# A grouped expert feed-forward kernel: weight loads move from once per expert to once per block, x arrives transposed, the work between the engines is dealt out anew

## The reference

```python
Wi_b = Wi[expert_idx]      # (E, 256, 1024) -> one per sample; bi, Wo (E, 1024, 256), bo, gamma, beta alike
h = gelu(einsum('bsh,bhi->bsi', x, Wi_b) + bi_b, approximate=False)
o = einsum('bsi,bih->bsh', h, Wo_b) + bo_b
r = o + x
y = (r - mean(r)) * rsqrt(var(r) + 1e-12)
return y * gamma_b + beta_b
```

## Time and profile before

| | |
|---|---|
| median of 3 runs | 149.77 us |
| the three runs | 149.15, 149.77, 151.67 us |
| span of the profiled execution, first to last instruction | 147.0 us |
| the median less that span (entry and exit) | 2.8 us |
| TensorE busy | 118.9 us (81%) |
| VectorE busy | 115.8 us (79%) |
| ScalarE busy | 76.2 us (52%) |
| GpSimd busy | 68.8 us (47%) |
| moved by DMA | 25.03 MB, 170 GB/s over the span |

### The profile page before, as it was taken

The page is one execution under the profiler, slowest core; times in us unless marked ns, Lnnn a source line. Parts: engine busy times, 40 slices in busy tenths (PEclk is TensorE's granted clock), DMA queues, the critical chain, the costliest instruction groups (busy, mean ns, idle before and its releaser), DMA issues.

```text
span 147.0 us, 3876 instructions
## 1 busy us (share of the span) xinstructions
PE 118.9 (81%) x949; PEld 116.1 (79%) x949; DVE 115.8 (79%) x181; ACT 76.2 (52%) x126; POOL 68.8 (47%) x57
## 2 busy tenths in 40 slices
PE   0296968998999999497999979993999399977800
PEld 0195968997999999496999979992999299977800
DVE  2493457178988998995999699969996999679880
ACT  3022966677089408547933990299129912970000
POOL 3006570217614962404492659255925593570220
PEclk9999999999999999999999999999999968999995
DMA  4979996999818210293947488756124612020021
GB/s 108 384 214 357 342 322 139 287 384 302 327 37 276 57 36 18 72 379 98 311 84 303 113 282 264 245 119 233 34 71 121 211 33 66 13 60 18 0 55 36
DMA packets 17710, 25.03 MB, mean 170 GB/s; under 512 B 1616, under 2 KB 14480, under 8 KB 17552
## 3 DMA queue, kind: packets, MB, share of 16 engines
q10 hardware_dynamic: 9824, 14.42, 30.3%
q1 hardware_dynamic: 7856, 10.26, 23.1%
HBM read 22.58 MB, written 2.10 MB: 168 GB/s over the span
## 4 chain that ended last, share of the span: by engine, by line
issue 50%; POOL 20%; DMA 12%; POOLq 7%; SPq 6%; DVE 2%; DVEq 0%; PE 0%
POOL wo_lo L344 14%; DMA x_in<-x_dram 6%; POOL xs L355 6%; DMA bo_bc<-L_cond_bo_dram 5%; SPq L214 5%; POOLq L224 3%; POOLq L355 1%; DMA idx_i<-itok_B_dram 1%; SPq L224 1%; POOL rstd L362 1%; POOLq L56 1%; SPq L181 0%; POOLq L373 0%; POOLq L383 0%; POOLq L372 0%
## 5 line engine op out<-in xcount | busy, mean ns | idle before, releaser
L344 POOL TENSOR_TENSOR wo_lo<-wo_in,wo_hi 128x1024 fp32r<-128x1024 f32 x15 | 43.7, 2932 | 22.7 <-ACT wo_hi L425 22.7
L696 PE MATMUL preact<-xT_hi,wi_hi 128*128 128x256 f32 x144 | 42.1, 292 | 11.6 <-DVE wi_lo L569 6.1
L436 ACT ACTIVATE h<-preact,biT 128x256 f32<-128x256 f32 x72 | 28.3, 484 | 41.3 <-DVE h_lo L596 29.2
L596 DVE TENSOR_TENSOR h_lo<-h,h_hi 128x512 fp32r<-128x512 f32 x36 | 47.4, 1357 | 0.6 <-ACT h_hi L444 0.6
L696 PE MATMUL preact<-xT_lo,wi_hi 128*128 128x256 f32 x144 | 41.5, 288 | 0.0
L696 PE MATMUL preact<-xT_hi,wi_lo 128*128 128x256 f32 x144 | 41.4, 288 | 0.0
L696 PEld LDWEIGHTS preact<-xT_hi,wi_hi 128*128 128x128 f32 x144 | 28.3, 196 | 13.0 <-issue 13.0
L696 PEld LDWEIGHTS preact<-xT_hi,wi_lo 128*128 128x128 f32 x144 | 28.4, 197 | 0.0
L696 PEld LDWEIGHTS preact<-xT_lo,wi_hi 128*128 128x128 f32 x144 | 28.3, 197 | 0.0
L713 PE MATMUL sums_ps<-wo_hi,h_hi 128*128 128x256 f32 x144 | 23.9, 288 | 1.7 <-DVE r L537 1.6
L362 POOL TENSOR_TENSOR rstd<-var_eps,minus_half 128x2 f32<-128x2 f32 x9 | 8.6, 953 | 34.7 <-DVE var_eps L550 34.7
(11 more groups left out here) (57 smaller groups left out, 74.9 us busy)
## 6 DMA issues: line engine op xcount, KB each, us to landing
wo_in<-L_cond_Wo_dram ACTq DMA_DIRECT2D x7, 1024.0 KB, 6.1
wi_in<-L_cond_Wi_dram ACTq DMA_DIRECT2D x5, 1024.0 KB, 5.2
wi_in<-L_cond_Wi_dram SPq DMA_DIRECT2D x3, 1024.0 KB, 9.4
x_in<-x_dram SPq DMA_DIRECT2D x36, 64.0 KB, 2.8
y_dram<-xs SPq DMA_DIRECT2D x32, 64.0 KB, 2.1
bo_bc<-L_cond_bo_dram SPq DMA_DIRECT2D x1, 1024.0 KB, 7.0
wo_in<-L_cond_Wo_dram SPq DMA_DIRECT2D x1, 1024.0 KB, 6.6
gamma_bc<-L_cond_gamma_dram ACTq DMA_DIRECT2D x3, 256.0 KB, 5.6
```

The lines of the kernel that those rows point to most:

```text
L344: nc.gpsimd.tensor_tensor(wo_half(wo_lo, e, half), wo_half(wo_in, e, half), wo_half(wo_hi, e, half).bitcast(FP32), ALU.subtract).then_inc( ...
L436: nc.scalar.activation(h[:, c, :], preact_chunk(c), ACT.Gelu, bias=biT[:, bass.ds(e * IC + c, 1)]).then_inc(gelu_done, 1)
L596: nc.vector.tensor_tensor(piece(h_lo, i), piece(h, i), piece(h_hi, i).bitcast(FP32), ALU.subtract).then_inc(h_lo_done, 1)
L696: last = nc.tensor.matmul(preact_chunk(c), w[:, e % 2, k, c * P:(c + 1) * P], xT[:, k, :], start=(k == 0 and w is wi_hi and xT is xT_hi), ...
```

## The change

- **Blocks unrolled.** The loops over experts and blocks become straight code for blocks 0 to 7 and nested conditions for the rest. Each block loads its own `wi`, `wo` and a row of parameters (`bo`, `gamma`, `beta`, `bi`), whether or not it shares the expert with the block ahead. The host lays the weights, parameters and x out in the order in which SBUF wants them.
- **x transposed.** The host gives x a second time, transposed (`x_columns`), so that TensorE's transposes and their PSUM bank go; each block loads four 64 KB pieces of it besides the four of `x_rows` for the residual.
- **Shorter sort.** Seven dependent steps with two waits for TensorE in place of fifteen. Table entries are now single sample numbers, read by one `value_load` each; places without a sample point to zero rows behind x, and every place is stored, with no conditions.
- **Queues.** All loads and stores of x, the weights and the parameters from the second block on are issued by SyncE; ScalarE's queue issues only the first block's `wi`, half of its x and its `wo`.
- **TensorE.** A quarter of the first product of block t (two chunks) alternates with a quarter of the second product of block t-1.
- **GELU in PSUM.** ScalarE writes GELU back to the bank it read; rounding (`h_high`) and subtraction (`h_low`) read PSUM. The SBUF copy `h` goes.
- **Subtractions.** `wo_lo` moves from GpSimd to VectorE; GpSimd keeps the residual bias and the root, now one per tile.

```diff
-            for (tile, half), b in samples.items():
-                eng.dma_start(x_tile(t, tile)[half * S:(half + 1) * S, :],
-                              x[bass.ds(b, 1), :, :].rearrange("o s h -> (o s) h")).then_inc(
-                                  first_x_loaded if is_first(t) else x_loaded, 16)
...
+        def entry(eng, at, hi, lo=0):
+            return eng.value_load(table[0:1, at:at + 1], min_val=lo, max_val=hi)
+
+        def sample(eng, t, j):
+            return entry(eng, QUAD * t + j, ROWS - 1)
...
+        def load_wi(eng, t, e):
+            if t >= 2:
+
+                eng.wait_ge(wi_lo_done, wi_count(t - 2, len(wi_pieces(t - 2)) - 1))
+            eng.dma_start(wi_in[:, t % 2, :, :, :].rearrange("p c k n -> p (c k n)"),
+                          wi[bass.ds(e, 1), :, :].rearrange("o p f -> (o p) f")).then_inc(wi_loaded[t % 2], 16)
...
+        def load_xT(eng, t, slots=range(QUAD)):
+            if t >= 2:
+                eng.wait_ge(x_ready, t - 1)
+            for j in slots:
+                b = sample(eng, t, j)
+                eng.dma_start(xT_in[:, t % 2, j, :, :].rearrange("p k s -> p (k s)"),
+                              xt[bass.ds(b, 1), :, :].rearrange("o p f -> (o p) f")).then_inc(xT_loaded[t % 2], 16)
+
+        def load_x(eng, t):
+            if t >= X_RING:
+                eng.wait_ge(stored[t % X_RING], 4 * loads_of(t - X_RING, X_RING))
+            for j in range(QUAD):
+                b = sample(eng, t, j)
+                eng.dma_start(slot(t, j), xr[bass.ds(b, 1), :, :].rearrange("o s h -> (o s) h")).then_inc(
+                    x_loaded[t % X_RING], 16)
+
+        def store(eng, t, tile):
+            eng.wait_ge(y_ready, 2 * t + tile + 1)
+            for j in (2 * tile, 2 * tile + 1):
+                b = sample(eng, t, j)
+                eng.dma_start(out[bass.ds(b, 1), :, :].rearrange("o s h -> (o s) h"), slot(t, j)).then_inc(
+                    stored[t % X_RING], 16)
...
+            sp.wait_ge(table_ready, 1)
+            load_xT(sp, 0, (0, 1))
+            second = expert(sp, 1)
+            load_wi(sp, 1, second)
+            load_xT(sp, 1)
+            load_params(sp, 1, second)
+            load_x(sp, 0)
+            load_wo(sp, 1, second)
+            load_x(sp, 1)
+            n = entry(sp, T_BLOCKS, MAX_BLOCKS, MIN_BLOCKS)
+
+            def iteration(t, ahead):
+                if ahead:
+                    e = expert(sp, t + 2)
+                    load_xT(sp, t + 2)
+                    load_wi(sp, t + 2, e)
+                    load_params(sp, t + 2, e)
+                    load_x(sp, t + 2)
+                if t >= 2:
+                    store(sp, t - 2, 1)
+                if ahead:
+                    load_wo(sp, t + 2, e)
+                if t >= 1:
+                    store(sp, t - 1, 0)
...
         @block.scalar
         def _(act):
...
+            def iteration(t, has_next):
+                gelu(t, 0)
+                if has_next:
+                    wi_high(t + 1, 0)
+                h_high(t, 0)
+                gelu(t, 1)
+                if has_next:
+                    wi_high(t + 1, 1)
+                h_high(t, 1)
+                gelu(t, 2)
+                wo_high(t, 0)
+                h_high(t, 2)
+                gelu(t, 3)
+                wo_high(t, 1)
+                h_high(t, 3)
...
         @block.vector
         def _(dve):
...
+            def h_low(t, q):
+                if q >= NS:
+                    return
+                dve.wait_ge(h_hi_done, NS * t + q + 1)
+                hi, lo = (x[:, t % 2, 2 * q:2 * q + 2, :].rearrange("p c n -> p (c n)") for x in (h_hi, h_lo))
+                nc.vector.tensor_tensor(lo, preact[:, q, :], hi.bitcast(FP32), ALU.subtract).then_inc(h_lo_done, 1)
...
+            def iteration(t, has_next, has=True):
+                if t >= 1:
+                    h_low(t - 1, 3)
+                    wo_low(t - 1, 1)
+                if t >= 2:
+                    centre(t - 2, 1)
+                if has:
+                    h_low(t, 0)
+                if t >= 2:
+                    finish(t - 2, 1)
+                if has_next:
+                    wi_low(t + 1, 0)
+                if has:
+                    h_low(t, 1)
+                if t >= 1:
+                    centre(t - 1, 0)
+                if has_next:
+                    wi_low(t + 1, 1)
+                if has:
+                    h_low(t, 2)
+                if t >= 1:
+                    finish(t - 1, 0)
+                if has_next:
+                    split_x(t + 1)
+                if has:
+                    wo_low(t, 0)
...
         @block.tensor
         def _(pe):
...
+            def iteration(t, _):
+                for q in range(4):
+                    first_product(t, q)
+                    if t >= 1:
+                        second_product(t - 1, q)
```

More of the change, by code:

```diff
@@ L485, in _, with end @@
+            def end(t):
+                act.nop()
+            for piece in range(4):
+                wi_high(0, piece)
+            for t in range(MIN_BLOCKS - 1):
+                iteration(t, True)
+            with_next(act, n, MIN_BLOCKS - 1, iteration, end)
         @block.vector
@@ L646, in _, with wi_low @@
-            for tile in range(2):
-                take_sums(blocks, tile)
-            normalise(blocks, very_last_expert)
+            n = entry(dve, T_BLOCKS, MAX_BLOCKS, MIN_BLOCKS)
+            def wi_low(t, piece):
+                a, b = wi_pieces(t)[piece]
+                dve.wait_ge(wi_hi_done, wi_count(t, piece))
+                nc.vector.tensor_tensor(flat(wi_lo, t, (a, b)), flat(wi_in, t, (a, b)), flat(wi_hi, t, (a, b)).bitcast(FP32),
+                                        ALU.subtract).then_inc(wi_lo_done, 1)
@@ L650, in _, with end @@
+            def end(t):
+                iteration(t, False, has=False)
+                centre(t - 1, 1)
+                finish(t - 1, 1)
+            wi_low(0, 0)
+            wi_low(0, 1)
+            split_x(0)
+            wi_low(0, 2)
+            wi_low(0, 3)
+            for t in range(MIN_BLOCKS - 1):
+                iteration(t, True)
+            with_next(dve, n, MIN_BLOCKS - 1, iteration, end)
         @block.tensor
         def _(pe):
-            pe.wait_ge(const_step, 8)
-            pe.wait_ge(sort_step, 2)
@@ new lines, in iteration, with end, kernel @@
+            def iteration(t, _):
+                for q in range(4):
+                    first_product(t, q)
+                    if t >= 1:
+                        second_product(t - 1, q)
+            def end(t):
+                for part in range(4):
+                    second_product(t - 1, part)
+            for t in range(MIN_BLOCKS):
+                iteration(t, True)
+            from_block(pe, n, MIN_BLOCKS, iteration, end)
+def kernel(x, itok_B_0_7, L0_cond_Wi, L0_cond_bi, L0_cond_Wo, L0_cond_bo, L0_cond_gamma, L0_cond_beta):
```

865 lines of the change are left out of this document (338 added, 527 removed).

## The result

The changed kernel takes 174.54 us (median of 4 runs, 172.06 to 175.49) against 149.69 us for the kernel before: a ratio of 1.161 (95% interval 1.150 to 1.172), slower. Times in this document are medians of all runs of a kernel, while ratios leave out the runs that are over 1.5% above that kernel's fastest; r1 and r9, where that leaves two of four, have no ratio. The forecast was 183 us with a range of 150 to 195. The profiled execution has a span of 172.4 us and a time of 174.45.

The account below looks back on a forecast made before the run. The prediction took SyncE's instruction stream as the bound: 27.6 us ahead of its iterations, iterations to 132.3, the last `wi` issued at 139.0, and compute and stores to a 180.6 us span; plus 2.8 gives 183 us, range 150 to 195.

Parts of the forecast that it names:

- SyncE's stream: SyncE's reads and issues in order: 18.8 us a full iteration against VectorE's 12.7, so it bounds the kernel; chance 0.79.
- One sign of the forecast: TensorE and VectorE busy for under two thirds of the span, idle for a DMA that SyncE issued late.
- The price of a transfer: On SyncE, one 64 KB transfer with its table read: 0.59 + 0.75 = 1.34 us, range 1.24 to 1.48.
- the sum: SyncE's start, its iterations, the last `wi` and the compute after it, added to a span of 180.6 us.
- From the last `wi` to the end: Last `wi` issued at 139.0 us, landing at 143.9; then block 8's products, normalisation and stores, to 180.6 us.
- The 2.8 us of entry and exit: Added to the span for the time: the median of the runs lay 2.8 us above the profiled span.
- VectorE's work: VectorE's operations in one block after the change: 12.35 us, or 12.7 with delays from GpSimd.
- The 0.35 us for GpSimd's additions: GpSimd's two 256-column additions a block can hold VectorE up: 0.35 us a block, range 0 to 1.5.
- both sums of the earlier trace: VectorE's sums with one input in PSUM, 0.41 and 0.42 us, said to run unharmed beside GpSimd's subtraction.
- The VectorE-bound one: Rival: SyncE's stream is not the bound, VectorE is; 136 us span, 139 us time (131 to 147); chance 0.15.
- Cheaper reads: Rival: bounds and assertion fall away on SyncE, a transfer costs 1.05 us; span 156 us, time 159 us; chance 0.06.
- `wo_low` on GpSimd costs 4.1 us a block: VectorE's `h_lo` waits for GpSimd's `wo_lo`, 5.37 - 1.28 = 4.1 us in each turn of an expert's first block.

Follow-up runs that it names:

- r1: The changed kernel with the sample numbers read for transposed x kept in registers for x's rows, 28 reads fewer on SyncE: 155.75 us.
- r9: r7 with 44 matrix products of a constant, with no reader, in TensorE's wait for block 1: 144.27 us.
- r3: The changed kernel with the four loads of x's rows a block issued by ScalarE's queue instead of SyncE: 146.40 us.
- r4: The changed kernel with the four loads of x's rows a block issued by GpSimd instead of SyncE: 148.79 us.
- r2: The changed kernel with only a quarter of `wi` (from block 2) and `wo` (from block 3) loaded, by as many issues: 169.68 us.
- b1: The kernel before with one edit, `wo_lo`'s subtraction moved from GpSimd to VectorE: 138.92 us.
- r5: r3 with `wo_low`'s subtraction given back to GpSimd: 184.21 us.
- r7: r3 with x's rounding copy on ScalarE and the first `wo` issued after the first two roundings of `wi`: 141.65 us.
- r10: r7 with block 1's x rounded and split ahead of the rest of block 0, and 34 unread constant products in TensorE's wait: 141.67 us.

## Why the prediction was right

**SyncE's stream is the bound.** Right, and shown: fewer reads (r1) or other issuers (r3, r4) remove the loss; a third fewer bytes (r2) doesn't. The rule by which issue time is usually small beside the transfer (the Trainium skill, DMA: Bandwidth & Descriptors, Issuing engines are not separate DMA queues) does not hold for this kernel: 1.28 us of stream for a 64 KB load that lands in a median of 3.1 us is small only where few stand in line, and here fifteen transfers a block do. One sign of the forecast did not come: TensorE was busy for 72% of the span, not under two thirds, because the half clock after its waits lengthened its work.

**The price of a transfer.** This is the term that was mis-sized, 1.34 us. Rows and stores took 1.27, pieces of transposed x 1.09, because their issue, which no trace of before had, is 0.33 us and not 0.48; the forecast priced both kinds as one. `wi` and the parameters took 0.52, not 0.7, and `wo`, not shown apart, more than that (its issue alone is 0.46 to 1.47 us). A full iteration is 17.3 us on average (the issues of `wi` at 58.88, 76.28, 92.99, 110.48 and 128.01) and not 18.8. The last `wi` was forecast for 139.0 us and issued at 128.01. That is 11.0 us too much; 1.9 us of it had arisen by block 2's `wi` (27.6 + 0.59 + 4 × 1.34 = 33.5, issued at 31.60), 8.3 in the six iterations between (forecast 104.7, measured 96.4), and 0.7 is the issue of the last `wi`, which the sum put ahead of its start. The shorter sort gave nothing: the first table read begins at 6.3 us (forecast 5.5; 5.79 before).

**From the last `wi` to the end.** Forecast 41.6 us (180.6 - 139.0), measured 44.4 (172.4 - 128.0). Block 8's first product came 14.9 us after the issue (forecast 14.3), and from there to the end it took 29.5 us (forecast 27.3). The sum priced all matrix instructions at 0.12 us; the granted clock over this stretch was 0.85. The two errors have opposite signs, and leave 8.2 us between the spans, 180.6 and 172.4; that the time came nearer than the transfer's price deserved is luck. The 2.8 us of entry and exit were a median less the span of another, quicker run; in the profiled run of the changed kernel they are 2.1 (174.45 - 172.4).

**VectorE's work.** Forecast 12.35 us a block, measured 11.85. The 0.35 us for GpSimd's additions don't show in the changed kernel, where VectorE has idle time; in r1 and r3, where it is full, it is busy for 12.7 us in most blocks with the same instructions. r3's timelines show where: in a block of 12.9 us GpSimd's additions (71.88 us, 1.61 us long) lie beside VectorE's last step and `wi_low`; in a block of 12.4 us, the last two rows, the additions begin at 85.56, behind the start of `wi_low`, and neither row is longer than usual.

```profile
72.01 0.88 DVE L511 SCALAR_TENSOR_TENSOR xs<-centred,rstd,params 128x256 f32<-128x256 f32 x1
72.81 1.76 DVE L465 TENSOR_TENSOR wi_lo<-wi_in,wi_hi 128x1024 fp32r<-128x1024 f32 x1
...
84.94 0.48 DVE L511 SCALAR_TENSOR_TENSOR xs<-centred,rstd,params 128x256 f32<-128x256 f32 x1
85.33 1.22 DVE L465 TENSOR_TENSOR wi_lo<-wi_in,wi_hi 128x1024 fp32r<-128x1024 f32 x1
```

So where they meet, the term is 0.9 us of VectorE's busy time and 0.5 us of the block. Taken together, 12.7 was forecast and 12.9 is the block that r3 shows. `h_low` was 0.68 to 0.69 us throughout, as forecast. The forecast took both sums of the earlier trace rows as run beside GpSimd's subtraction; the one at 108.14 starts after that had ended (101.30 + 6.37 = 107.67). The one at 117.34 does run beside the next, which the trace of the kernel before has at 116.06, 3.63 us long.

**The rivals.** The VectorE-bound one was wrong for the changed kernel and right as a mechanism behind it. Its time, 139 us, was too short by 7: r3 has its blocks of 12.9 us and takes 146.4. Of the 8.8 us between the spans (136 and 144.8) the start has 8.5: the first product begins at 14.7 us (forecast 12), block 0 lasts 11.6 (8) and block 1 14.9 (12.7). Full DMA engines until 40 us and the half clock in block 1 were not in the forecast; how they share the 8.5 us was not told apart. Cheaper reads (159 us) did not happen: each of the 115 reads has its load, its bounds and its assertion, 0.57 us. The single load is 0.27 us at the median here too, against the floor of about 600 ns that the Trainium skill gives (DMA: Bandwidth & Descriptors, Latency and other measured facts).

**What was not in it.** That `wo_low` on GpSimd costs 4.1 us a block was read from one turn of before, and b1 gives 10.8 us for the edit. That the same edit is worth 38 us in r3's layout (r5) was not foreseen: the wait falls on another instruction, one that TensorE stands directly behind, and brings the half clock with it.

**Left open.** GELU in PSUM was not undone alone; r5 shows what it shields, not what it is worth while `wo_low` is on VectorE. Nor was the shorter sort, or loading weights per block, tried alone. How r1 would go with more blocks, once SyncE's lead is used up, was not run.

## What to carry to other kernels

Add up the instruction stream of each engine that issues transfers like any other engine's work: here a read of a table word, its bounds, an address and an issue came to 1.1 to 1.3 us, and the product of that with the transfers of a block decided the time, though no busy share showed it. The cure is cheap where another queue has room: keep the register instead of reading again, or deal the issues out. Before a rebuild of a whole kernel, try its parts one by one: one moved subtraction, alone, was worth 10.8 us, more than the best of the ten kernels built on the rebuild gained (8.1 in r7, 8.4 in r10).

## What the runs showed of the hardware

- **A copy with one input in SBUF was held up by GpSimd's subtraction**: 2.56 us against 0.42 (median of nine, r5 and r3), while a subtraction with one input in PSUM stayed at 0.68. The forecast had looked only at VectorE's two-input instructions. The Trainium skill (SBUF — State Buffer, Who interferes with whom) says that a copy or a cast can run in a mode that takes the ports shared with GpSimd, and that whichever engine issues first then holds them for its whole instruction while the other is blocked. The trace agrees as far as it goes: GpSimd's subtractions began at 93.73 and ended at 99.21 us, the copy began at 96.94 and ended at 99.50.
- **TensorE's clock after a wait.** After its wait of 3.60 us in the changed kernel TensorE came back at a granted clock of 0.50 (1.2 of 2.4 GHz). Its windows behind that wait:

```profile
108.00:109.00 1.00, 1.00 (x7) 1.00 (x6) 1.00 (x3) 0.00 (x0) 0.00 (x0) 0.50 0.20 58
...
110.00:112.00 2.00, 2.00 (x15) 2.00 (x15) 1.50 (x6) 0.81 (x2) 0.71 (x2) 0.80 0.33 68
112.00:114.00 2.00, 2.00 (x19) 2.00 (x18) 0.00 (x0) 0.00 (x0) 1.41 (x3) 1.00 0.92 360
```

  The starts of its matrix instructions lie 0.21 us apart instead of 0.12 there, and this raises TensorE's busy time from 11.7 to 13.2 us a block, so that a busier TensorE here is a sign of waiting. That the wait is what takes the clock is shown by r9 and r10, where fillers in the wait kept it at 1.00. In the changed kernel, with its bound elsewhere, it cost some 3 us (the estimate under r1); in r5 TensorE's busy time was 12.4 us above r3's.
- **Two shapes of transfer had issues of different length**: for the same 64 KB, SyncE's issue took 0.33 us as 128 pieces of 512 bytes and 0.48 us as 64 rows of 1 KB, at the median of 34 and 36 issues. That the shape is the reason was not tried alone.
